# Spare products ahead of two stages, another queue for the first weights, another order of units, squares summed on ScalarE

## What is computed

```python
h   = einsum('bni,di->bnd', layernorm(x), W) + b
att = sigmoid((h @ a1)[:, :, None] + (h @ a2)[:, None, :] + att_b) * adj   # masked, rows divided by their sum
x   = x + einsum('bij,bjd->bid', att, h)
xn  = layernorm(x)
topk_vals, topk_idx = top_k(xn @ gate_w + gate_b, 2)
topk_w = softmax(topk_vals)
hid = relu(einsum('bsh,ehf->bsef', xn, w1) + b1)           # 16 experts, hidden 256
sel = take_along_axis(einsum('bsef,efh->bseh', hid, w2) + b2, topk_idx)
y   = xn + sum(topk_w * sel, over the two)
out = x + layernorm(y) * gamma + beta
```

## Time and profile before

| | |
|---|---|
| profiled execution, its own time | 460.95 us |
| its span (first to last instruction) | 459.2 us |
| mean granted TensorE clock | 0.902 of full speed |
| busy: TensorE, VectorE, ScalarE, GpSimd | 335.4, 304.1, 220.8, 302.5 us |
| last scatter starts | 208.11 us |
| first product of the experts | 216.55 us |
| first send | 225.43 us |
| first addition of the last stage | 416.64 us |

### The profile page before, as it was taken

The page is one execution under the profiler, slowest core; times in us unless marked ns, Lnnn a source line. Parts: engine busy times, 40 slices in busy tenths (PEclk is TensorE's granted clock), DMA queues, the critical chain, the costliest instruction groups (busy, mean ns, idle before and its releaser), DMA issues.

```text
span 459.2 us, 11050 instructions
## 1 busy us (share of the span) xinstructions
PE 335.4 (73%) x2259; PEld 276.0 (60%) x2259; DVE 304.1 (66%) x1482; ACT 220.8 (48%) x592; POOL 302.5 (66%) x331
## 2 busy tenths in 40 slices
PE   4678868877788764100999999989898989707891
PEld 3567757766778653100887787777777778603330
DVE  4686999999999974600476666666555556502895
ACT  3569869888999744100333333333333334401431
POOL 6520767777777777771277777777777777760565
PEclk9999989999999955555899999999999999956997
DMA  7812635545565722596767777777777775219974
GB/s 243 273 57 71 195 128 187 177 165 165 157 209 169 255 105 106 173 244 198 218 178 209 216 218 214 215 225 222 216 223 218 218 229 166 77 35 344 337 282 137
DMA packets 61682, 88.09 MB, mean 192 GB/s; under 512 B 10213, under 2 KB 40859, under 8 KB 61490
## 3 DMA queue, kind: packets, MB, share of 16 engines
q1 hardware_dynamic: 32370, 44.89, 33.1%
q0 software_dynamic: 10720, 25.32, 15.6%
q10 hardware_dynamic: 18528, 17.19, 12.7%
HBM read 55.61 MB, written 32.73 MB: 192 GB/s over the span
## 4 chain that ended last, share of the span: by engine, by line
PE 22%; DVE 20%; ACTq 15%; issue 14%; ACT 9%; DMA 5%; SPq 4%; POOL 3%; DVEq 0%; POOLq 0%
PE psum L1263 6%; ACTq L598 5%; ACTq L283 5%; PE psum L1252 4%; ACTq L282 4%; ACT hid L603 4%; ACT xn L532 3%; DMA out_dram<-xrow 3%; POOL token_y L442 3%; PE psum L1165 2%; DVE i L839 2%; PE psum L1155 2%; DVE xrow L1066 2%; SPq L333 1%; DVE xmid L759 1%
## 5 line engine op out<-in xcount | busy, mean ns | idle before, releaser
L442 POOL DMA_INDIRECT token_y<-yb,xb x143 | 142.9, 999 | 59.7 <-issue 40.6
L419 POOL DMA_INDIRECT sorted_x<-xrow,rows x128 | 123.4, 964 | 59.8 <-issue 56.1
L603 ACT ACTIVATE hid<-psum,b_sb 128x256 f32<-128x256 f32 (+1 forms) x188 | 69.2, 419 | 142.9 <-PE psum L1252 64.0
L1263 PE MATMUL psum<-w_sb,hid 128*128 x572 | 83.4, 283 | 11.3 <-ACT hid L603 10.4
L1263 PEld LDWEIGHTS psum<-w_sb,hid 128*128 128x128 f32 x572 | 74.7, 192 | 21.0 <-issue 18.2
L1252 PE MATMUL psum<-xbT,w_sb 128*128 128x256 f32 (+1 forms) x376 | 82.1, 342 | 2.5 <-DVE xbT L1016 2.3
L1025 DVE TENSOR_TENSOR yb<-psum,b_bc 128x256 f32<-128x256 f32 x94 | 33.9, 360 | 63.5 <-PE psum L1263 59.4
L1252 PEld LDWEIGHTS psum<-xbT,w_sb 128*128 128x128 f32 x376 | 58.0, 194 | 8.0 <-DVE xbT L1016 4.8
L1242 PE MATMUL psum<-ident_aug,xb 128*128 128x128 f32 x143 | 33.3, 290 | 24.0 <-DMA xb<-sorted_x 22.1
L1016 DVE COPY xbT<-psum 128x256 f32<-128x256 f32 x94 | 33.2, 353 | 23.5 <-PE psum L1242 23.4
L1030 DVE SCALAR_TENSOR_TENSOR yb<-yb,xb 128x128 f32<-128x128 f32 x143 | 46.3, 352 | 3.4
(11 more groups left out here) (166 smaller groups left out, 555.1 us busy)
## 6 DMA issues: line engine op xcount, KB each, us to landing
xb<-sorted_x SPq DMA_DIRECT2D x49, 258.0 KB
w_sb<-w_dram ACTq DMA_DIRECT2D x83, 128.0 KB
adj_in<-adj_dram SPq DMA_DIRECT2D x32, 256.0 KB
got<-token_y SPq DMA_DIRECT2D x16, 512.0 KB, 6.2
xb<-sorted_x SPq DMA_DIRECT2D x45, 129.0 KB
out_dram<-xrow ACTq DMA_DIRECT2D x16, 256.0 KB, 3.1
w_sb<-w_dram SPq DMA_DIRECT2D x27, 128.0 KB
xmid<-x_dram SPq DMA_DIRECT2D x6, 512.0 KB, 8.8
```

The costliest lines, as they stand in the source:

```text
L419: pool.indirect_dma_start(sorted_x, bass.IndirectOffsetOnAxis(ap=rows[:, slot, t, k:k + 1], axis=0), xrow[:, slot, k, t, :], None).then_in ...
L442: pool.indirect_dma_start(token_y, bass.IndirectOffsetOnAxis(ap=xb[:, q, t, TO:TO + 1].bitcast(I32), axis=0), yb[:, h, t, :], None, bounds ...
L603: last = act.activation(hid[:, u % RING, c, 0:n], psum[:, 2 + u % 2, c * BT:c * BT + n], ACT.Relu, bias=b1_sb[:, c, e])
L1263: last = mm(psum[:, 4 + u % 2, t * D:(t + 1) * D], hid[:, u % RING, c, t * P:(t + 1) * P], w2_sb[:, e, c * D:(c + 1) * D].rearrange("p a c ...
```

## The change

Four things change.

1. The first weights of units 0 to 10 are loaded by ScalarE's queue, behind its fills and ahead of its first relu, instead of by SyncE.
2. `ORDER` begins with two 128-row units; TensorE does transpose and layer 1 of unit 0, then of unit 1, then layer 2 of unit 0, before it goes on as it did; VectorE's `unit_y(0)` stands ahead of `unit_x(2)`.
3. `hold_clock(n)` issues n products of the unit matrix with 512 columns of second weights, into a PSUM bank that nothing reads. Twenty stand behind the landing of pair 14's scatters and four behind pair 15's, ahead of the first unit. Behind the last unit stands one for each tile of the last eight units, each behind the landing of that unit's sends, and two more.
4. In the last stage ScalarE squares each tile of 128 columns by itself and writes the sum of the squares into PSUM in the same instruction; VectorE's sums go. The root reads these sums.

```diff
+LEAD = 2
+ORDER = (tuple(FULL + i for i in range(LEAD)) + tuple(range(AHEAD + LEAD))
+         + tuple(b for i in range(LEAD, TAILS) for b in (AHEAD + i, FULL + i)))
...
-            for u in range(IN_RING):
-                load_w1(sp, u)
...
             act.wait_ge(table_done, 1)
+            for u in range(IN_RING):
+                load_w1(act, u)
             act.wait_ge(b1_in, 16)
...
-                if g >= 2:
-                    act.wait_ge(square_sums, g - 1)
-                act.activation(squares[:, g % 2, :, :].rearrange("p t c -> p (t c)"), psum[:, g % CBANKS, :], ACT.Square
-                               ).then_inc(squared, 1)
+                for t in range(GT):
+                    n = g * GT + t
+                    if n >= 2:
+                        act.wait_ge(square_sums, n - 1)
+                    act.activation(squares[:, t % 2, :], psum[:, g % CBANKS, t * D:(t + 1) * D], ACT.Square,
+                                   accum_out=sums_v[:, g % CRING, t:t + 1]).then_inc(square_sums, 1)
...
-                v.tensor_reduce(rs3[:, g % CRING, 0, :], squares[:, g % 2, :, :], axis=AX, op=ALU.add).then_inc(square_sums, 1)
...
+            def hold_clock(n):
+
+                for _ in range(n):
+                    mm(hold_ps, ident[:, :], w2_sb[:, 0:2, :].rearrange("p e c -> p (e c)"), start=True, stop=True)
+
+            pe.wait_ge(h_sb_g, 2 * PAIRS)
+            for i, n in ((PAIRS - 2, 20), (PAIRS - 1, 4)):
+                pe.wait_ge(scattered[i % XROWS], free_after(i) + 16 * SCATTERS)
+                hold_clock(n)
...
+            for u in range(UNITS - OUT_RING, UNITS):
+                pe.wait_ge(yb_out[u % OUT_RING], 16 * sent(u, OUT_RING))
+                hold_clock(tiles_of(u))
+            hold_clock(2)
```

More of the change, by code:

```diff
@@ L54 @@
 AHEAD = FULL - TAILS
-ORDER = tuple(range(AHEAD)) + tuple(b for i in range(TAILS) for b in (AHEAD + i, FULL + i))
+LEAD = 2
+ORDER = (tuple(FULL + i for i in range(LEAD)) + tuple(range(AHEAD + LEAD))
+         + tuple(b for i in range(LEAD, TAILS) for b in (AHEAD + i, FULL + i)))
+assert sorted(ORDER) == list(range(UNITS))
 IN_RING = 11
@@ L214, in build @@
         got = sb("got", [P, GOT_RING, GT, TOPK, D])
-        squares = sb("squares", [P, 2, GT, D])
-        rs3 = sb("rs3", [P, CRING, 3, GT])
+        squares = sb("squares", [P, 2, D])
+        rs3 = sb("rs3", [P, CRING, 2, GT])
         z = xrow[:, 0, :, :, :].rearrange("p k t c -> p (k t c)")[:, 0:CRING * GT * D].rearrange(
@@ L227, in build @@
         total_v = route_ps[:, 2 * TPP * EXPERTS:(2 * TPP + 1) * EXPERTS]
+        sums_v = psum[:, CBANKS + 2, 0:CRING * GT].rearrange("p (q t) -> p q t", t=GT)
+        hold_ps = psum[:, CBANKS + 3, :]
         weights_in, consts_in, late_in = sem("weights_in"), sem("consts_in"), sem("late_in")
@@ L257, in build @@
         got_in = [sem(f"got_in{q}") for q in range(GOT_RING)]
-        summed, squared, square_sums, std_done, z_done, res_done = (
-            sem("summed"), sem("squared"), sem("square_sums"), sem("std_done"), sem("z_done"), sem("res_done"))
+        summed, square_sums, std_done, z_done, res_done = (
+            sem("summed"), sem("square_sums"), sem("std_done"), sem("z_done"), sem("res_done"))
         res_out = [sem(f"res_out{q}") for q in range(CRING)]
@@ L616, in square @@
                 act.wait_ge(summed, g + 1)
-                if g >= 2:
-                    act.wait_ge(square_sums, g - 1)
-                act.activation(squares[:, g % 2, :, :].rearrange("p t c -> p (t c)"), psum[:, g % CBANKS, :], ACT.Square
-                               ).then_inc(squared, 1)
+                for t in range(GT):
[4 more added lines that the diff above has]
+                                   accum_out=sums_v[:, g % CRING, t:t + 1]).then_inc(square_sums, 1)
             def deviation(g):
                 q = g % CRING
-                act.wait_ge(square_sums, g + 1)
-                act.activation(rs3[:, q, 1, :], rs3[:, q, 0, :], ACT.Sqrt, bias=eps_t[:, :], scale=1.0 / D).then_inc(std_done, 1)
+                act.wait_ge(square_sums, (g + 1) * GT)
+                if g >= CRING:
+                    act.wait_ge(z_done, g - CRING + 1)
+                act.activation(rs3[:, q, 0, :], sums_v[:, q, :], ACT.Sqrt, bias=eps_t[:, :], scale=1.0 / D).then_inc(std_done, 1)
             def store_group(g):
@@ L1043, in _ @@
             for u in range(UNITS + 2):
+                if u == 2:
+                    unit_y(0)
                 if u < UNITS:
                     unit_x(u)
-                if u >= 2:
+                if u >= 3:
                     unit_y(u - 2)
@@ L1049, in _ @@
                     add_beta(u // 3)
-            def add_squares(g):
-                dve.wait_ge(squared, g + 1)
-                if g >= CRING:
-                    dve.wait_ge(std_done, g - CRING + 1)
-                v.tensor_reduce(rs3[:, g % CRING, 0, :], squares[:, g % 2, :, :], axis=AX, op=ALU.add).then_inc(square_sums, 1)
             def scale(g):
@@ L1060, in scale @@
                 dve.wait_ge(std_done, g + 1)
-                n = step(v.reciprocal(rs3[:, q, 2, :], rs3[:, q, 1, :]))
+                n = step(v.reciprocal(rs3[:, q, 1, :], rs3[:, q, 0, :]))
                 dve.wait_ge(dve_step, n)
@@ L1066, in scale @@
                     last = v.scalar_tensor_tensor(out=z[:, q, t, :], in0=psum[:, g % CBANKS, t * D:(t + 1) * D],
-                                                  scalar=rs3[:, q, 2, t:t + 1], in1=gamma_bc[:, :], op0=ALU.mult, op1=ALU.mult)
+                                                  scalar=rs3[:, q, 1, t:t + 1], in1=gamma_bc[:, :], op0=ALU.mult, op1=ALU.mult)
                 last.then_inc(z_done, 1)
-            for g in range(GROUPS + 1):
-                if g < GROUPS:
-                    add_squares(g)
-                if g:
-                    scale(g - 1)
+            for g in range(GROUPS):
+                scale(g)
         @block.tensor
@@ L1272, in _ @@
             pe.wait_ge(h_sb_g, 2 * PAIRS)
-            e1 = e2 = None
-            for u in range(UNITS + 2):
+            e2, e1 = expert_of(0), expert_of(1)
+            turn_x(0)
+            layer1(0)
+            turn_x(1)
+            layer1(1)
+            layer2(0, e2)
+            for u in range(2, UNITS + 2):
                 e0 = expert_of(u) if u < UNITS else None
@@ L1277, in _ @@
                     turn_x(u)
-                if 1 <= u <= UNITS:
+                if 3 <= u <= UNITS:
                     layer1(u - 1)
-                if u >= 2:
+                if u >= 3:
                     layer2(u - 2, e2)
```

## The result

The changed kernel took 467.88 us (median of 4 runs, 465.98 to 469.11); the kernel before took 462.2 beside it. The ratio is 1.0126 (95% interval 1.0082 to 1.0169): slower by more than 0.5%, inside the range of the prediction and 1.9 us above its number. The profiled execution took 465.98 us, with a span of 464.2 and a mean granted clock of 0.931.

A forecast was written before the change was run, and what follows sets the result against it. GpSimd's sends were taken to bound the expert stage, ScalarE the changed last stage. Span 459.2 + 4.0 (experts) + 0.0 (last stage) = 463.2, execution 464.95, median 466.6, stated as 466 us; range 459 to 474.

The forecast's parts named there:

- The direction and the place: Whole kernel: slower, chance 0.66, with +4.0 us from a later first send of the expert stage.
- I take 201: Ahead of the expert stage: pair 14's last scatter, started at 197.99, lands at 201 us; bounds 200.1 to 203.
- the expert term: Expert stage: first send counts as if at 229.4 against 225.43, +4.0 us; bounds +0.8 to +7.2.
- First send and starvation: Expert stage's start: 3.6 us from free TensorE to first send, then GpSimd runs dry twice, 1.8 us in all.
- It counts in full: Expert stage: GpSimd's 1.8 us of starvation reaches the end whole, as GpSimd has no other gap to give back.
- First weights at nothing: Ahead of experts: moving 11 weight loads to ScalarE costed at nothing; 2.8 us gain hidden by spare products until 224.
- The last stage: Last stage: 0.0 us in all, the gained clock included; -5 with a step of 0.26, +10.9 with 0.57.
- I take 0.40: Last stage: ScalarE's step per 128-column square with its sum is 0.40 us; bounds 0.26 and 0.57.
- It becomes the bound: Last stage: ScalarE, at 2.2 us a group, sets the pace over TensorE's 1.72 and VectorE's 1.3.
- The rival with nearly free sums: Last stage: -5 us if a square with its sum steps at 0.28 or less; chance 0.14.
- The end products hold the clock: Before the last stage: fourteen products keep the clock up, gaining 1.85 us at its head; rival that they don't, 0.06.
- The two cancel: Whole kernel: a square step near 0.30 gives 3 to 4 us, late first send takes 4; 461 to 463.5, chance 0.20.

The follow-up runs named there:

- eight buffers: Eight buffers for scaled results instead of four, in the version with twenty spare products at once, old unit order and weights five units ahead: 452.64 us.
- split weights: Changed kernel with nine front products, old unit order, five first weights loaded at once and six behind the last scatters' landing: 455.94 us.
- no products, five ahead: Changed kernel without front spare products, with the old unit order and layer-1 weights loaded five units ahead throughout: 456.29 us.

## Why the prediction was right, and where it was wrong

*The direction and the place: right.* The spare products in front are what makes it slower. Undoing them alone brings 467.88 to 458.06, and starting them earlier brings it to 458.7. Their length was forecast at 23.0 us and is 22.98, with a rise of the clock after 4.3 us (4.5 taken).

*The landing of pair 14: the step that failed in front.* "I take 201" is 3.0 us after the scatter's start; it landed 7.04 us after it, at 204.6, outside the bounds of 200.1 to 203. This is 3.7 of the 4.8 us that the expert term is short. In the six other profiles that wait for it, it took 8.6 to 10.3. I had taken the landing of a send that had the DMA engines to itself and allowed at most 3 us more, but in that time fills, scatters and weights keep the DMA engines busy without a pause. The stretch of the changed kernel from 198 to 205, DMA share in the last column but one:

```profile
198.00:205.00 7.00, 0.25 (x1) 0.28 (x2) 0.00 (x0) 0.00 (x0) 5.34 (x6) 0.50 1.13 218
```

The share is 1.13, against 0.19 in a stretch with one of the last sends. That the load is the cause is argued and not shown, as no run takes it away from pair 14. The landings go with the share over their own length: 2.09 us at 0.10 (the last send of the kernel before), and for pair 15's last scatter 2.45 at 0.32 (eight buffers), 3.31 at 0.45 (split weights) and 5.67 at 0.97 (no front products), but 4.67 at 0.43 (no products, five ahead). The scatter that landed in 2.45 came behind seven others at the usual step, so these alone don't make a landing late.

The Trainium skill, "DMA: Bandwidth & Descriptors", section "Anatomy of one DMA — SWDGE (gpsimd) path", gives such a DMA a fixed part of about 2 us that scales with nothing, beside a part for the bytes it moves. The last send's 2.09 us agree with it; the 7.04 of a loaded stretch lie far above, and the measurement decides.

*First send and starvation: sizes off.* From the end of the products to the first send it was 232.40 - 227.73 = 4.7 us (3.6 taken): transposes, copies and hand-overs of the second unit stand between. The two gaps cost 1.49 + 1.07 = 2.6 (1.8 taken, bound 2.4). That is 1.1 + 0.8 more, and GpSimd's other steps took 0.8 less (184.5 us without the gaps, 185.2 before): 3.7 + 1.1 + 0.8 - 0.8 = 4.8, and 4.0 + 4.8 = 8.8. Whether that 0.8 answers "It counts in full" stays open: in the six other profiles with two lead units these steps took 185.0 to 186.2, so it may be chance of this execution.

*First weights at nothing: right, for another reason.* There was next to nothing to hide. The statement that without cover they would be worth 2.8 us is wrong: with nine products or none, the rows are asked for 6.0 to 6.5 us after the last scatter starts, and with the loads back on SyncE 6.4, with a median within 0.3 us. In the changed kernel's own profile it is 212.14 - 207.69 = 4.5, so with the loads in the same place this distance varies by some 2 us from one profile to the next. The landing of the scatters took SyncE's place; that the eleven transfers are a part of it fits the run with six of them held back, and is not shown beyond that variation.

*The last stage: the forecast was wrong and its rival right.* "I take 0.40" for a square with its sum measures 0.25, below the bound of 0.26. The store's issue, 0.38 of the 0.6 beside the squares, costs nothing. So "It becomes the bound" fails: ScalarE needs 1.25 us a group, not 2.2, and TensorE's 1.72 decides. By the prediction's own test (a step under 0.3) that part of it was wrong. The rival with nearly free sums had priced the stage at -5, with 2 us already taken back by waits for stores; it came to -3.8. Both its terms are seen: 1.8 at the head, since the first addition takes 427.16 - 425.34 = 1.82 in place of 3.57, and then TensorE's step of 1.72 for as long as buffers are free. From the fifth group on VectorE waits 0.7 to 1.2 us a group for a store, seven times, and from the ninth on TensorE's step grows to (453.49 - 437.46) / 8 = 2.0. With eight buffers this goes too.

*The end products hold the clock: right.* The gaps of 0.7 to 1.1 us between them did not let it fall.

So the sum came out within 1.9 us by luck: an error of +4.8 in one term met one of -3.8 in the other. The rival "The two cancel" was closer to the mechanism than the forecast; the landing decided that they did not.

## What to carry to other kernels

Spare work that holds a clock must end when the real work arrives: let it start behind something early and certain, and count it from the rise of the clock on. Behind a landing under load its length begins only when that landing comes: 24 products there cost some ten us, nine showed no cost. That a clock that is up in front is worth anything on the whole time was not shown here. Before moving DMA issues to another queue, ask whether the issuing engine or the landing of something else is the last to come; here the other queue showed nothing in the times (0.3 us), and six transfers fewer beside the awaited one at most 1.0. And where an engine becomes faster in a pipeline, look at once for the buffers that the next wait is for: here four more of them gave 2.0 us of the stage, and the summed squares 1.1.

## What was not expected of the hardware

- An indirect DMA that lands in 2.09 us alone needed 7.0 to 10.3 us for pair 14, beside fills and weights, and it varies by that much from one profile to the next; spare products tied to it move with it.
- A square with its sum is a square and a separate read of 0.18 us, but the read overlaps: 0.22 to 0.25 us from square to square, no more than the plain step of the relu of that size (0.26, worked out from the earlier trace rows).
- The clock rose 4.3 us after work began in front of the changed kernel, 5.9 us after it at the last stage of the run without end products, and 3.6 in the kernel before at the same place: a rise can't be taken from one trace closer than that.
